# A fused layer kernel on one core: the second half of y is transposed into another PSUM bank, and a dozen steps get new places

## Chip, cores and metric

The kernel runs on one core of a Trainium2 chip. The metric is the device time of one launch in microseconds (us). A core has five engines that this text names: TensorE (PE in the profile; PEld are its weight loads), VectorE (DVE), ScalarE (ACT), GpSimd (POOL) and SyncE (SP), which here only issues DMAs. Each runs its own instructions in the order in which they are written. They wait for each other by semaphores.

## What is computed

Three blocks over x of 2 x 2048 tokens by 1024 features, each added to x:

```
x = x + 0.5 * ffn(layernorm(x))
x = x + attn(layernorm(x))
x = x + 0.5 * ffn(layernorm(x))

ffn:   vecs[s,a,r] = A[a,r,:] . x[s]          a = 64 experts, r = 16
       the 4 experts with the largest |vecs[s,a,:]| get route 1/4
       v[s,r] = sum_a routes[s,a] * vecs[s,a,r]
       out = x W^T + bias + sum_a,r routes[s,a] * B[a,:,r] * v[s,r]
attn:  xz = x W_xproj^T -> delta_r (128), B (16), C (16)
       delta = softplus(delta_r W_dt^T + b_dt)
       h_t = exp(delta_t * A) * h_(t-1) + delta_t * B_t * x_t     (1024 features x 16 states)
       y_t = sum_n h_t * C_t ;  out = y + x * D
```

## The kernel before

**Units.** The work is cut into 64 units of 128 tokens by `plan`. A unit of kind 1 is a tile of the first ffn, and a unit of kind 2 is a tile of the last one. Units 0 to 13 are of kind 1, units 14 to 47 alternate (with two of kind 1 in a row at 29 and 30, and at 46 and 47), and units 48 to 63 are of kind 2. Through units 5 to 57 the scan of the middle block runs beside them: 256 groups of 4 scans over 512 tokens, 5 groups in most units and 4 in nine of them (5, 10, 16, 22, 28, 34, 40, 46 and 52). In a unit, a is the unit itself, b the one behind it, and l the one ahead of it.

**The names in a unit.** TensorE makes three products of a 128-token tile, each 48 matmuls of 512 columns, in two halves (nb) and thirds of 8 matmuls: `experts` (pv<-wA,xT), made for b at the end of unit a; `base` (po<-wW,xT); `routed` (po<-wB,uT). ScalarE squares the expert vectors (`squares`, L773), VectorE adds them up (`sums`, L998) and finds the four largest (`choose`), ScalarE writes the mask (L777), and VectorE forms the gathered and masked vectors (`gather`, L1014 to L1025, through pv). SyncE turns them by DMA into uT (L344). VectorE adds each half of the result to xin (`result`, L1030). For b, VectorE takes the statistics (`unit_stats`, L971), ScalarE normalises (xn, L760), TensorE transposes xn into bank 0 of pv and into pt (`norm_blocks`, L481), ScalarE rounds these to xT's high part (`high`, L765), and VectorE takes the low part (`low_part`, L994). `experts(b, nb=0)` waits with its first third for both high parts and the first low part, and with its last third for the second low part.

**Kind 1 has more.** Its result is normalised again at the end of the unit (`stats("ln2")`, `normed2`, L783). In the next unit, where it is l and called late, TensorE transposes this into pt (`scan_blocks`), multiplies it with wx (`scan_products`, L616, into bank 0 of pv), and transposes the product (`turn_products`, L622).

**Kind 2 takes y.** Where b is of kind 2, TensorE transposes the y that the scan made for it in two halves (`y_blocks`), and VectorE adds each to xin (`add_y`, L980). This is so in units 13, 15, 17, 19, 21, 23, 25, 27, 30, 32, 34, 36, 38, 40, 42, 44 and 47 to 62.

**The scan.** ScalarE makes one decay tile for each scan (L843, `decays`; decay i waits until scan i-2 is done, since pA has two banks), VectorE scans (L1050), GpSimd multiplies by B before (L444, L449) and by C behind it (L457), and TensorE sums over states (`states`, L647). Every 16 scans need a delta tile: `z` (L634) on TensorE, `magnitudes` and `softplus` on ScalarE, `delta` (L1037, L1040; it reads a tile of x that SyncE loads) on VectorE, `delta_copy` (L825) and `delta_out` (L834) on ScalarE, a store to DRAM and loads from there. `plan` gives z to places 0 and 1 of a unit. Units 5, 10, 15, 20, 25, 30, 34, 39, 44, 49 and 54 have both (double units below). Of the other scan units, 6, 7, 11, 12, 16, 17, 21, 26, 31, 35, 36, 40, 41, 45, 46, 50 and 55 have place 1 alone, unit 57 has none, and the rest have place 0 alone.

All places within a unit are written out by hand, engine by engine: `decays(lo, hi)` and `scans(lo, hi)` say which scans of the unit stand there, and the other calls stand between them.

## Time and profile before

| | before |
|---|---|
| median of 3 runs (lowest to highest) | 2925.07 us (2923.59 to 2925.81) |
| the profiled execution | 2920.77 us, span 2919.0 us |
| mean granted TensorE clock | 0.976 |

The rows further down come from the one profiled execution. Its span is the time from the first to the last instruction. The time that the runs report has 1.77 us around it. Rows of the timeline give the start in us from the span's start, the duration in us, the engine, the line, the operation and how many instructions were merged; where the engine stood idle ahead of it, the idle time and what ended it stand in brackets.

### The profile page before, as it was taken

Reading aid. Unit: us, or ns where it says so; the run is one execution under the profiler, and the core shown is the slowest. Engines: PE = TensorE matmul, PEld = TensorE weight load, DVE = VectorE, ACT = ScalarE, POOL = GpSimd, SP = SyncE. Lnnn points to the kernel's source line nnn. Section 1 sums busy time; section 2 is a strip of 40 time slices with the busy share of each in tenths; the row PEclk is TensorE's granted clock in tenths of the full one; section 3 lists DMA queues with packets and bytes.
Section 4 is the critical chain, followed back from the end, with each engine's and each line's share of the span. In section 5 each row is a group of like instructions: output and inputs, shape, how many; then the busy total and the mean of one; then the engine's idle time right before and its main releaser. Section 6 shows DMA issues by size and latency. Waiting matters only on the chain.

```text
span 2919.0 us, 38379 instructions
## 1 busy us (share of the span) xinstructions
PE 2621.1 (90%) x13056; PEld 1164.8 (40%) x13120; DVE 2278.2 (78%) x2917; ACT 1425.2 (49%) x2819; POOL 2347.1 (80%) x703
## 2 busy tenths in 40 slices
PE   4997999999889898889899899899899888988999
PEld 1453444444343344344334334344334333333444
DVE  8435888788878879888888888888797888888533
ACT  5224565555545455554555555555555544454211
POOL 2003999899989999999899899989999899989200
PEclk8999999999999999999999999999999999999999
DMA  5225445544445445544454345344544444344221
GB/s 212 59 61 128 129 132 134 162 139 131 130 136 159 113 122 145 153 126 131 131 163 141 116 126 171 115 135 129 156 136 146 123 147 144 107 133 120 66 58 51
DMA packets 309370, 373.42 MB, mean 128 GB/s; under 512 B 148147, under 2 KB 224051, under 8 KB 309174
## 3 DMA queue, kind: packets, MB, share of 16 engines
q1 hardware_dynamic: 292278, 337.40, 39.2%
q10 hardware_dynamic: 16896, 33.56, 3.8%
q8 instruction: 104, 1.70, 0.2%
q14 instruction: 92, 0.75, 0.1%
HBM read 234.05 MB, written 103.29 MB: 116 GB/s over the span
## 4 chain that ended last, share of the span: by engine, by line
PE 18%; DVE 18%; DVEq 8%; DMA 7%; issue 4%; ACT 4%; POOL 3%; SPq 1%; ACTq 1%; POOLq 0%
DVE mreg L1050 9%; PE po L489 5%; PE pv L489 5%; PE pv L493 3%; PE po L493 3%; DVEq L1052 2%; DMA delta_scratch<-mreg 2%; DMA xin<-x_scratch 2%; DVE pv L1017 2%; DMA mreg<-xnT_scratch 2%; POOL mreg L457 2%; ACT pA L843 1%; DVE sel L1025 1%; DVEq L1016 1%; POOL mreg L449 1%
## 5 line engine op out<-in xcount | busy, mean ns | idle before, releaser
L457 POOL TENSOR_TENSOR mreg<-mreg 128x2048 f32<-128x2048 f32 x256 | 1161.4, 4538 | 30.8 <-DVE hst L1053 30.8
L843 ACT ACTIVATE pA<-mreg,nA 128x512 f32<-128x512 f32 x1024 | 696.1, 687 | 745.9 <-DVE mreg L1050 658.9
L449 POOL TENSOR_TENSOR mreg<-mreg 128x1024 f32<-128x1024 f32 x340 | 795.2, 2364 | 285.3 <-DMA mreg<-delta_scratch 276.6
L1050 DVE TENSOR_TENSOR_SCAN mreg<-pA,hst,mreg 128x512 f32<-128x512 f32 x768 | 941.5, 1265 | 55.1 <-ACT pA L843 43.8
L489 PE MATMUL pv<-wA,xT 128*128 128x512 f16 x2016 | 465.8, 385 | 51.8 <-DVE xT L994 24.4
L489 PE MATMUL po<-wB,uT 128*128 128x512 f16 x2016 | 463.8, 381 | 24.6 <-DVE xin L980 13.1
L489 PE MATMUL po<-wW,xT 128*128 128x512 f16 x2016 | 467.2, 380 | 8.0 <-issue 7.0
L444 POOL TENSOR_TENSOR mreg<-mreg 128x2048 f32<-128x2048 f32 x86 | 390.3, 4539 | 4.1 <-issue 4.1
L489 PEld LDWEIGHTS pv<-wA,xT 128*128 128x128 f16 x2016 | 195.2, 99 | 334.0 <-issue 63.1
L1050 DVE TENSOR_TENSOR_SCAN mreg<-pA,cst,mreg 128x512 f32<-128x512 f32 x256 | 313.5, 1265 | 17.9 <-ACT pA L843 17.6
L489 PEld LDWEIGHTS po<-wB,uT 128*128 128x128 f16 x2016 | 190.8, 98 | 318.8 <-issue 77.0
L998 DVE TENSOR_REDUCE n<-sel 128x32 f32<-128x512 f32 x128 | 85.3, 684 | 263.1 <-ACT sel L773 262.8
L489 PEld LDWEIGHTS po<-wW,xT 128*128 128x128 f16 x2016 | 197.9, 98 | 222.1 <-issue 8.5
L647 PE MATMUL py<-mreg,Em 128*32 128x512 f32 x2048 | 274.5, 608 | 13.0 <-POOL mreg L457 12.4
L493 PE MATMUL pv<-wA,xT 128*128 128x512 f16 x1008 | 244.3, 386 | 22.1 <-DVE xT L994 22.1
L493 PE MATMUL po<-wW,xT 128*128 128x512 f16 x1008 | 253.3, 397 | 0.0
L493 PE MATMUL po<-wB,uT 128*128 128x512 f16 x1008 | 239.9, 381 | 0.0
L1030 DVE SCALAR_TENSOR_TENSOR xin<-po,sc,xin 128x512 f32<-128x512 f32 x128 | 94.5, 738 | 87.1 <-PE po L493 83.2
L493 PEld LDWEIGHTS pv<-wA,xT 128*128 128x128 f16 x1008 | 99.1, 99 | 147.1 <-issue 33.5
L493 PEld LDWEIGHTS po<-wW,xT 128*128 128x128 f16 x1008 | 97.3, 101 | 151.1 <-issue 59.1
L493 PEld LDWEIGHTS po<-wB,uT 128*128 128x128 f16 x1008 | 99.0, 98 | 106.0 <-issue 1.7
L773 ACT ACTIVATE sel<-pv 128x512 f32<-128x512 f32 x128 | 72.3, 584 | 131.3 <-PE pv L493 131.2
(129 smaller groups left out, 2387.5 us busy)
## 6 DMA issues: line engine op xcount, KB each, us to landing
mreg<-delta_scratch SPq DMA_DIRECT2D x256, 512.0 KB, 5.7
delta_scratch<-mreg ACTq DMA_DIRECT2D x128, 256.0 KB
xin<-x SPq DMA_DIRECT2D x32, 512.0 KB, 4.6
x_scratch<-xin SPq DMA_DIRECT2D x32, 512.0 KB, 7.4
xnT_scratch<-auxs SPq DMA_DIRECT2D x32, 512.0 KB, 2.9
mreg<-xnT_scratch SPq DMA_DIRECT2D x64, 256.0 KB, 6.9
mreg<-bc_scratch SPq DMA_DIRECT2D x64, 256.0 KB, 6.0
yT_scratch<-mreg SPq DMA_DIRECT2D x64, 256.0 KB, 2.3
```

The costliest lines, as they stand in the source:

```text
L444: pool.tensor_tensor(Hr[:, G % NH, :, :], u, b.broadcast_to([P, 4, CT]), ALU.mult).then_inc(s_bm, 2)
L449: pool.tensor_tensor(Hr[:, G % NH, 2 * h:2 * h + 2, :], u, b.broadcast_to([P, 2, CT]), ALU.mult).then_inc(s_bm, 1)
L457: pool.tensor_tensor(h, h, Cr[:, g, :].unsqueeze(1).broadcast_to([P, 4, CT]), ALU.mult).then_inc(s_cm, 1)
L489: last = nc.tensor.matmul(dst, lhs[:, 0, k, :], w[:, wb, k, nb * HF:(nb + 1) * HF], start=(first and k == 0 and wb == 0), stop=False)
L493: last = nc.tensor.matmul(dst, lhs[:, 1, k, :], w[:, 0, k, nb * HF:(nb + 1) * HF], start=False, stop=(stop and k == KD - 1))
L647: last = nc.tensor.matmul(py[32 * s:32 * s + 32, :], Em[:, :], Hr[:, G % NH, s, :], start=(g == 0), stop=(g == 3), tile_position=(0, 32 * s))
L773: nc.scalar.activation(sel[:, nb * HF:(nb + 1) * HF], pv[:, nb, :], ACT.Square).then_inc(s_sq, 1)
L843: nc.scalar.activation(pA[:, i % 2, :], Dr[:, 2 * (n % NPR) + i % 2, :], ACT.Exp, scale=nA[:, c:c + 1]).then_inc(s_dA, 1)
L998: V.tensor_reduce(n2[:, nb * NE // 2:(nb + 1) * NE // 2], sel3[:, nb * NE // 2:(nb + 1) * NE // 2, :], AX.X, ALU.add)
L1017: V.tensor_reduce(pvs, sel[:, :].rearrange("p (a r) -> p r a", r=R16), AX.X, ALU.add)
L1030: V.scalar_tensor_tensor(dst, po[:, nb, :], sc[:, 3:4], dst, ALU.mult, ALU.add).then_inc(s_res, 1)
L1050: V.tensor_tensor_scan(h, pA[:, i % 2, :], h, before, ALU.mult, ALU.add).then_inc(s_sc, 1)
```

## The change

There are two parts. The second half of y goes to bank 0 of pv instead of pt, so it no longer waits for the first `add_y` (s_ya) but for the unit's `gather` (s_u), which uses that bank. `scan_products`, which writes that bank too, waits for both `add_y` where there is a y. And a dozen calls stand at new places on TensorE, ScalarE and VectorE.

```diff
+        pty = (pt[:, :], pv[:, 0, :])
...
                 else:
-                    pe.wait_ge(s_ya, b.v * 2 + 1)
-                blocks(pt, lambda k: auxy[:, half * KB + k, :], s_yT, idf[:, :])
+                    pe.wait_ge(s_u, b.u * 2)
+                blocks(pty[half], lambda k: auxy[:, half * KB + k, :], s_yT, idf[:, :])
...
TensorE, unit():
-                z(a, 0)
                 if late:
                     scan_blocks(late, 1)
+                z(a, 0)
                 base(a, 1, 0)
                 if y:
                     if late:
                         pe.wait_ge(s_nc, late.w * 2 + 2)
                     y_blocks(y, 0)
-                if late:
-                    scan_products(a, late)
-                base(a, 1, 1)
                 if y:
                     y_blocks(y, 1)
+                base(a, 1, 1)
                 base(a, 1, 2)
                 states(a, 1)
+                if late:
+                    scan_products(a, late, y)
...
+                routed(a, 0, 0)
                 if late:
                     turn_products(late)
-                routed(a, 0, 0)
                 routed(a, 0, 1)
...
ScalarE, unit():
-                decays(2, 3)
                 if late:
                     scan_input_copies(late, 1)
-                decays(3, 4)
+                decays(2, 4)
                 magnitudes(a, 0)
+                decays(4, 7)
                 softplus(a, 0)
-                decays(4, 8)
+                decays(7, 8)
                 if late:
                     projections(late)
                 decays(8, 9)
+                delta_copy(a, 0)
                 if late:
                     projection_copies(late)
                 decays(9, 10)
-                delta_copy(a, 0)
                 delta_out(a, 0)
...
+                if b:
+                    squares(b, 0)
                 decays(19, 20)
                 if a.kind == 1:
                     normed2(a, a.u * 2 + 4)
                 decays(20, 22)
-                if b:
-                    squares(b, 0)
...
VectorE, unit():
-                scans(4, 7)
+                scans(4, 5)
                 if b and b.kind == 2:
                     add_y(b, 1)
+                scans(5, 7)
                 delta(a, 0)
                 scans(7, 10)
                 if b:
                     unit_stats(b)
-                scans(10, 12)
                 result(a, 0)
-                scans(12, 15)
+                scans(10, 14)
                 if b:
                     low_part(b, 0)
+                scans(14, 15)
                 delta(a, 1)
+                scans(15, 16)
                 if b:
                     low_part(b, 1)
-                scans(15, 17)
+                scans(16, 18)
                 result(a, 1)
-                scans(17, 18)
                 delta(a, 2)
                 if a.kind == 1:
                     ...
                     stats("ln2", xin[:, a.p, :], s_mv2)
+                if b:
+                    sums(b, 0)
                 scans(18, 20)
-                if b:
-                    sums(b, 0)
```

TensorE, middle of a unit whose b is of kind 2 (uT is here the buffer that holds y, L481 before and L482 now its transposes). Before:

```order
L489 MATMUL po<-wW,xT 128x512 x8
L481 MATMUL pt<-idf,uT 128x128 [waits s_ldy]
L481 MATMUL pt<-idf,uT 128x128 x3
L489 MATMUL po<-wW,xT 128x512 x8
L481 MATMUL pt<-idf,uT 128x128 [waits s_ya]
L481 MATMUL pt<-idf,uT 128x128 x3
L493 MATMUL po<-wW,xT 128x512 x8
L647 MATMUL py<-mreg,Em 32x512 [waits s_y,s_cm]
L647 MATMUL py<-mreg,Em 32x512 x3
L489 MATMUL po<-wB,uT 128x512 [waits s_uc0,s_ya]
```

and now:

```order
L490 MATMUL po<-wW,xT 128x512 x8
L482 MATMUL pt<-idf,uT 128x128 [waits s_ldy]
L482 MATMUL pt<-idf,uT 128x128 x3
L482 MATMUL pv<-idf,uT 128x128 [waits s_u]
L482 MATMUL pv<-idf,uT 128x128 x3
L490 MATMUL po<-wW,xT 128x512 x8
L494 MATMUL po<-wW,xT 128x512 x8
L650 MATMUL py<-mreg,Em 32x512 [waits s_y,s_cm]
L650 MATMUL py<-mreg,Em 32x512 x3
L490 MATMUL po<-wB,uT 128x512 [waits s_uc0,s_ya]
```

The second four transposes moved ahead of the second third of base, and their wait is for the gather.

TensorE, the same stretch of a late unit, from the half of base on. Before:

```order
L567 MATMUL po<-brow,onesb 128x512 [waits s_res]
L489 MATMUL po<-wW,xT 128x512 x8
L616 MATMUL pv<-wx,auxs 128x160 [waits s_u,s_nc]
L616 MATMUL pv<-wx,auxs 128x160 x7
L489 MATMUL po<-wW,xT 128x512 x8
L493 MATMUL po<-wW,xT 128x512 x8
L647 MATMUL py<-mreg,Em 32x512 [waits s_y,s_cm]
L647 MATMUL py<-mreg,Em 32x512 x3
L622 MATMUL pv<-idf,xn 128x128 [waits s_pk,s_nc]
L623 MATMUL pv<-idf,xn 32x128
L489 MATMUL po<-wB,uT 128x512 [waits s_uc0]
```

and now:

```order
L568 MATMUL po<-brow,onesb 128x512 [waits s_res]
L490 MATMUL po<-wW,xT 128x512 x16
L494 MATMUL po<-wW,xT 128x512 x8
L650 MATMUL py<-mreg,Em 32x512 [waits s_y,s_cm]
L650 MATMUL py<-mreg,Em 32x512 x3
L619 MATMUL pv<-wx,auxs 128x160 [waits s_u,s_nc]
L619 MATMUL pv<-wx,auxs 128x160 x7
L490 MATMUL po<-wB,uT 128x512 [waits s_uc0,s_nc]
L490 MATMUL po<-wB,uT 128x512 x7
L625 MATMUL pv<-idf,xn 128x128 [waits s_pk]
L626 MATMUL pv<-idf,xn 32x128
```

The product with wx moved behind base and states, and the turning of its result behind the first third of routed.

VectorE, behind the statistics for b (L1050 and L1054 are the scans, L994 and L998 the low parts, L1030 and L1034 the two results, L1062 and L1066 a sum for y). Before:

```order
L973 BN_AGGR ln_mv<-ln_st 128x2
L1050 SCALAR_TENSOR_TENSOR mreg<-pA,hst,mreg 128x512 [waits s_dA] x2
L1053 TENSOR_REDUCE hst<-mreg 128x4
L1030 SCALAR_TENSOR_TENSOR xin<-po,sc,xin 128x512 [waits s_out]
L1050 SCALAR_TENSOR_TENSOR mreg<-pA,hst,mreg 128x512 [waits s_dA,s_sv,s_bm]
L1050 SCALAR_TENSOR_TENSOR mreg<-pA,hst,mreg 128x512 [waits s_dA] x2
L994 TENSOR_TENSOR xT<-pv,xT 128x512 [waits s_xhi]
L994 TENSOR_TENSOR xT<-pt,xT 128x512 [waits s_xhi]
L1050 SCALAR_TENSOR_TENSOR mreg<-pA,hst,mreg 128x512 [waits s_dA]
L1053 TENSOR_REDUCE hst<-mreg 128x4
```

and now:

```order
L977 BN_AGGR ln_mv<-ln_st 128x2
L1034 SCALAR_TENSOR_TENSOR xin<-po,sc,xin 128x512 [waits s_out]
L1054 SCALAR_TENSOR_TENSOR mreg<-pA,hst,mreg 128x512 [waits s_dA] x2
L1057 TENSOR_REDUCE hst<-mreg 128x4
L1054 SCALAR_TENSOR_TENSOR mreg<-pA,hst,mreg 128x512 [waits s_dA,s_sv,s_bm]
L1054 SCALAR_TENSOR_TENSOR mreg<-pA,hst,mreg 128x512 [waits s_dA]
L998 TENSOR_TENSOR xT<-pv,xT 128x512 [waits s_xhi]
L1054 SCALAR_TENSOR_TENSOR mreg<-pA,hst,mreg 128x512 [waits s_dA] x2
L1057 TENSOR_REDUCE hst<-mreg 128x4
L998 TENSOR_TENSOR xT<-pt,xT 128x512 [waits s_xhi]
```

The first low part stands one scan earlier, the second one scan later, and the first result two scans earlier.

## Rows read from the trace of the kernel before

**Rows 1.** The page's parts 1 and 2: busy us, share, instructions; granted clock
```profile
PE 2621.1 (90%) x13056; PEld 1164.8 (40%) x13120; DVE 2278.2 (78%) x2917; ACT 1425.2 (49%) x2819; POOL 2347.1 (80%) x703
...
PEclk8999999999999999999999999999999999999999
```

**Rows 2.** The page's part 4, the chain that ended last, by engine
```profile
PE 18%; DVE 18%; DVEq 8%; DMA 7%; issue 4%; ACT 4%; POOL 3%; SPq 1%; ACTq 1%; POOLq 0%
```

**Rows 3.** Waits, whole span: waiting instruction, releaser; total us, times, longest
```profile
POOL mreg L449 <- DMA mreg<-delta_scratch: 276.6, 29, 175.3
...
PE pt L481 <- DVE xin L980: 55.8, 23, 4.7
...
DVE mreg L1040 <- DMA mreg<-xnT_scratch: 52.6, 11, 5.9
PE pv L616 <- DVE sel L1025: 49.4, 30, 4.0
...
PE pv L489 <- DVE xT L994: 24.4, 22, 1.2
...
PE pv L489 <- ACT xT L765: 23.6, 12, 2.4
...
PE pv L481 <- ACT xn L760: 20.9, 15, 10.0
...
DVE xin L980 <- DMA xin<-x_scratch: 17.0, 6, 6.3
...
DVE mreg L1050 <- POOL mreg L449: 9.2, 8, 2.1
```

**Rows 4.** Timeline of unit 24, a late unit of kind 2 with z at place 0
```profile
1139.93 0.26 ACT L777 ACTIVATE mask<-n2m 128x64 f32<-128x64 f32 x1 [1.70 <-DVE n2m L1009]
...
1148.50 2.41 PE L616 MATMUL pv<-wx,auxs 128*128 128x160 f32 x16 [1.54 <-DVE sel L1025]
...
1163.73 1.25 ACT L760 ACTIVATE xn<-xin,ln_nm,ln_r 128x1024 f32<-128x1024 f32 x1
...
1165.68 3.64 DVE L1050 TENSOR_TENSOR_SCAN mreg<-pA,hst,mreg 128x512 f32<-128x512 f32 x3 [0.53 <-ACT pA L843]
...
1168.16 0.59 ACT L765 ACTIVATE xT<-pt 128x512 f16<-128x512 f32 x1
...
1170.04 3.61 PE L489 MATMUL pv<-wA,xT 128*128 128x512 f16 x16 [0.99 <-DVE xT L994]
...
1182.79 0.26 ACT L777 ACTIVATE mask<-n2m 128x64 f32<-128x64 f32 x1 [1.59 <-DVE n2m L1009]
```

**Rows 5.** Timeline of unit 23, of kind 1, whose b takes y
```profile
1105.41 0.66 PE L481 MATMUL pt<-idf,uT 128*128 128x128 f32 x4 [3.17 <-DVE xin L980]
...
1118.85 1.24 ACT L760 ACTIVATE xn<-xin,ln_nm,ln_r 128x1024 f32<-128x1024 f32 x1
...
1120.14 0.66 PE L481 MATMUL pv<-idf,xn 128*128 128x128 f32 x4 [0.70 <-ACT xn L760]
...
1134.80 1.24 ACT L783 ACTIVATE xn<-xin,ln_nm,ln_r 128x1024 f32<-128x1024 f32 x1
...
1137.17 1.05 ACT L773 ACTIVATE sel<-pv 128x512 f32<-128x512 f32 x2
```

**Rows 6.** Timeline of unit 25, a double unit of kind 1
```profile
1201.85 0.58 ACT L825 ACTIVATE mreg<-pv 128x512 f32<-128x512 f32 x1
...
1220.55 0.69 DVE L1040 TENSOR_TENSOR mreg<-pv,mreg 128x512 f32<-128x512 f32 x1 [4.43 <-DMA mreg<-xnT_scratch]
```

**Rows 7.** Timeline of unit 2, ahead of the scan
```profile
142.62 2.41 PE L616 MATMUL pv<-wx,auxs 128*128 128x160 f32 x16 [0.61 <-DVE sel L1025]
```

**Rows 8.** Timeline of unit 60, behind the scan
```profile
2795.88 1.22 DVE L1025 TENSOR_TENSOR sel<-mask,pv 128x1024 f16<-128x1024 f32 x1
...
2798.49 2.62 SPq L344 DMA_TRANSPOSE uT<-sel  x2
...
2801.86 3.61 PE L489 MATMUL po<-wB,uT 128*128 128x512 f16 x16 [1.72 <-DMA uT<-sel]
```

More of the change, by code:

```diff
@@ L607, in scan_blocks, with scan_products @@
                 blocks(pt, lambda k: xn[:, (half * KB + k) * P:(half * KB + k + 1) * P], s_nT, idf[:, :])
-            def scan_products(a, l):
+            def scan_products(a, l, y):
+                if y:
+                    pe.wait_ge(s_ya, y.v * 2 + 2)
                 if l.w == 0:
@@ L694, in unit @@
                 routed(a, 1, 2)
+                states(a, 3)
                 z(a, 2)
-                states(a, 3)
                 if b:
@@ L885, in unit @@
                     normed(b, 2 * (a.f1s - (a.kind == 1)))
-                decays(12, 14)
+                decays(12, 13)
+                decays(13, 14)
                 magnitudes(a, 1)
@@ L979, in add_y @@
                 dst = xin[:, b.p, half * HF:(half + 1) * HF]
-                V.tensor_tensor(dst, pt[:, :], dst, ALU.add).then_inc(s_ya, 1)
+                V.tensor_tensor(dst, pty[half], dst, ALU.add).then_inc(s_ya, 1)
             def unit_stats(b):
@@ L1106, in unit @@
                     stats("ln2", xin[:, a.p, :], s_mv2)
-                scans(18, 20)
                 if b:
                     sums(b, 0)
+                scans(18, 20)
             def combine():
```

## The prediction, made before the changed kernel was run

> **What bounds the kernel now.** I read the page first. TensorE has the most busy time, 90% of the span, and GpSimd and VectorE have 80% and 78% [rows 1]. The weight loads, at 40%, are no limit. GpSimd's 2347.1 us over 256 groups are 9.17 us a group, so 45.8 us for a unit with five groups. The granted clock is at its upper level nearly throughout [rows 1], so it gives the change nothing to win.
>
> The chain that ended last comes second: TensorE and VectorE have 18% of it each, GpSimd 3% [rows 2]. So no engine bounds the whole. A unit is a loop: mask, gather, ten scans, statistics, xn, transposes, high and low parts, experts for b, squares, the next mask. What stands last in that loop decides.
>
> The waits come third, with the two that the change is aimed at: TensorE waits 55.8 us for the first `add_y` before it turns the second half of y, and 49.4 us for the gather before the product with wx [rows 3]. I then followed one unit of each sort along the timeline to see what becomes of that time.
>
> *Late unit of kind 2* (unit 24, 42.86 us from mask to mask). TensorE waits 1.54 us at L616. But xn is done at 1163.73 + 1.25 = 1164.98, and TensorE takes it in its next matmuls at once. The next three scans end at 1169.32, the low parts follow, and experts start at 1170.04 after a wait of 0.99 for the first of them [rows 4]. TensorE's lost time at L616 has therefore only 0.3 us to give; xn comes from VectorE and ScalarE.
>
> *Unit of kind 1 with y* (unit 23). TensorE loses 3.17 us at the second half of y, and still waits 0.70 us for xn, which ends at 1120.09 [rows 5]. The end of the unit is set by the second normalisation: it ends at 1136.04, two decays follow, then both squares at 1137.17 [rows 5]. TensorE's experts had ended before that. So this unit is VectorE's and ScalarE's.
>
> *Double unit* (unit 25). The copy of the first delta ends at 1202.43, its store has to land, SyncE loads the second z's tile only behind that, and VectorE stands 4.43 us before L1040 [rows 6]; over the kernel it is 52.6 us in 11 double units [rows 3].
>
> **The change part by part.**
>
> *y's second half in pv, product with wx behind base and states.* In unit 23 TensorE would wait for the end of the gather, some 1.5 us, instead of 3.17, and its matmuls up to xn come some 2 us earlier. In late units the 1.6 us on average (49.4 / 30) go. What is behind both is the wait for xn, which grows by as much: before xn, VectorE's work between gather and statistics is the same two additions, one delta and eight scans in another order. I take 0 for all scan units; if that cover were gone, the price would be the 105 us of the two waits, less the new wait of 1.5 us in 30 units or so, which gives 60.
>
> Ahead of the scan there is no such cover: TensorE hardly waits there, and 0.61 us at L616 go in units 1 to 4 [rows 7]. That is 2.4 us. Behind the scan, in units 58 to 62, the turning into uT was issued at 2798.49, behind the second half of y, and routed waits 1.72 us for it [rows 8]. Now the gather's last write ends at 2795.88 + 1.22 = 2797.10, four transposes of some 0.6 us follow, and SyncE issues at 2797.8. That is 0.65 us sooner in 5 units, so 3.3 us.
>
> *The first low part one scan earlier.* In unit 24 it could start when the scan before the third ends, 1.2 us sooner (3.64 / 3), so at 1168.1. The second high part runs from 1168.16 to 1168.75 [rows 4] and experts want it too; the first one ends just ahead of it, and the low part behind that takes some 0.7 (as L1040 does, 0.69 [rows 6]) and ends at 1168.9. With 0.2 from there to the first matmul, experts start at about 1169.1 instead of 1170.04: 0.9 us. It counts only where experts set the end of the unit (kind 2), and only where no softplus lies between the two high parts. With z at place 1 the second high part comes later and already is what TensorE waits for (12 waits, 23.6 us, against 22 of 1.1 us for the low part [rows 3]). So it counts in 14 units: 14, 18, 22, 24, 28, 33, 37, 43, 48, 51, 52, 53, 56, 57. 14 x 0.9 = 12.6 us.
>
> *The second low part one scan (with place 1: two scans and a delta) later.* It is wanted by the third 3.6 us behind the start of experts [rows 4]. From 1168.3 on VectorE has 0.6 + 1.2 + 1.4 + 0.6 = 3.8 us until it ends, 1172.1, and TensorE wants it at 1172.7. With z at place 1, experts start later by the softplus (1.4), and the low part by a delta (1.4), which leaves some 0.4 us. I take 0. In the double units of kind 2 (20, 39, 49, 54) it is late by a scan, but TensorE then also waited there for the copy of delta, which comes sooner by that scan; 0.
>
> *One square and one sum ahead of the last scans.* In kind 1, both squares (1.05 us) stood behind the second xn. Now one stands there, which saves 0.5 us. Against it, VectorE waits some 0.3 for the high part, and the second statistics come later by that. My count of unit 23 gives a mask between 0 and 0.5 us earlier. In 20 single units of kind 1 I take 0.12 each, 2.5 us; both ends, 0 and 10, go to the range.
>
> *The copy of delta ahead of decay 9.* The store is issued some 0.5 us sooner, since ScalarE copies (0.58, [rows 6]) while it would wait for scan 7. The stand before L1040 ends sooner by that, in 7 double units of kind 1: 3.5 us. In the four of kind 2 the later low part takes it.
>
> *What takes back.* A shorter loop moves towards GpSimd, whose pace does not change. VectorE waits little for it now (9.2 us), but it waits 6 times, 17.0 us, for an xin that SyncE issues behind loads which wait for GpSimd [rows 3]. Where units before that got shorter, this wait grows by as much. I take 4 us.
>
> Sum: 12.6 + 2.5 + 3.5 + 2.4 + 3.3 - 4 = 20.3 us. The profiled execution took 2920.77 us, so 2900.5. The median of the three runs lies 4.3 us above it; from it the forecast is 2904.8 us.
>
> **The Trainium skill on this.** The page Perfetto Trace Analysis (Identifying the Most-Contended Engine) says to go by occupancy and to optimise the engine that has most of it, but it warns that busy matmul time is a poor measure, and to take the weight loads' share. By its strategy one closes the gaps on that engine; that is the first rival below, and by it the sum would be some 60 us larger. The trace agrees with the warning: 90% and 40% stand side by side.
>
> **The rivals.**
>
> *TensorE is the bound after all.* Its 90% speak for it. Against it are 0.70 us of wait for xn in unit 23 even after the 3.17. It would give about 60 us and the 20 of my sum, and GpSimd's waits bound it, since its work does not shrink: 276.6 - 175.3 = 101.3 us for delta, apart from the longest, which is the one ahead of the scan [rows 3]. Time: 2845 to 2870. Chance 0.09. A part of it, 30 to 50 us less than before, because the earlier turning lets SyncE go on sooner to the loads: 2875 to 2893, chance 0.16.
>
> *GpSimd takes it all back.* Unit 24, with five groups, already took 2.9 us less than the 45.8 that GpSimd needs for them, and only longer units make up for it. If the scans come to wait for GpSimd as soon as a unit is shorter, only the 5.7 us outside the scan stay. 2919 to 2925, chance 0.13. Against it stand the 101.3 us that it waits for delta.
>
> *The second low part is late (slower).* In 28 units with z at place 1 (17 single and 11 double) it has 0.4 us of slack by my count, behind a delta that waits for ScalarE. If delta ends over 0.4 us later than I think, TensorE stands before its last third, and so does ScalarE, where the square now stands ahead of decay 19: a scan and a delta wait of 1.4 us each. 28 x 1.4 = 39, less the 20 of my sum: 2944. Chance 0.09. From 0.7 us of wait per unit on (20 / 28) it makes the kernel slower.
>
> **How the numbers follow.** My case has a chance of 0.53 with 2893 to 2918; the part above 0.16; the whole of TensorE's waits 0.09; GpSimd 0.13; the late low part 0.09. Two runs of this kernel can be told apart from about 0.2%, 5.85 us. Faster by more: 0.53 + 0.16 + 0.09 = 0.78. Same: 0.13. Slower: 0.09. The range of 8 in 10 leaves out the late low part and most of TensorE's case, 2875 to 2922.
>
> **What would show it.** TensorE's waits for xin before the transposes of y and for the gather before the product with wx are gone, and its waits for xn (now 20.9 us [rows 3]) grow by about as much. TensorE's wait for the low part at L489 falls from 24.4 us to under 8. Units like 24 take 42.0 instead of 42.9, and units like 23 stay within 0.5 us. The double units get some 0.5 us shorter. Waits before the last third of experts stay below 30 us. The prediction is wrong if waits for xn do not grow (TensorE was the bound), if VectorE comes to wait for GpSimd by more than 20 us, or if the wait at the last third of experts exceeds 40.

## The result, and the profile after

| | before | changed |
|---|---|---|
| median of 5 runs (lowest to highest) | 2925.81 us (2923.59 to 2929.73) | 2909.53 us (2902.43 to 2911.2) |
| ratio, 95% interval | | 0.9945 (0.9931 to 0.9959) |
| profiled execution's span | 2919.0 us | 2900.6 us |

The change makes the kernel 16 us faster, where 20 were forecast. Timed again later beside the kernel before, it was 12 us faster (ratio 0.9956, 0.9941 to 0.997). The profiled execution of the changed kernel is its fastest run, 7 us below its median; the one of the kernel before is 5 us below its own, so the profiles flatter the difference by some 2 us. A second profile of the changed kernel, taken later, has a span of 2905.0 us; where the two differ, both are told.

The page of the changed kernel, part 1, and the chain that ended last by engine (part 4):

```profile
PE 2629.8 (91%) x13056; PEld 1167.3 (40%) x13120; DVE 2277.7 (79%) x2917; ACT 1422.9 (49%) x2819; POOL 2347.1 (81%) x703
...
PE 29%; DVE 29%; DVEq 12%; DMA 11%; issue 7%; ACT 5%; POOL 5%; SPq 1%; ACTq 1%; POOLq 0%
```

The engines do the same work as in [rows 1], in less time. The shares of [rows 2] add up to only 64% of the span, since that chain could not be followed back to the start; 18% of it each for TensorE and VectorE are 28% of what was followed, so the chain goes through both in equal parts as before (26% and 30% in the second profile). The waits over the whole span, in the form of [rows 3]:

```profile
POOL mreg L450 <- DMA mreg<-delta_scratch: 259.0, 25, 171.6
...
PE pv L482 <- ACT xn L763: 69.0, 38, 10.0
...
DVE mreg L1044 <- DMA mreg<-xnT_scratch: 50.0, 11, 5.9
...
PE pv L490 <- ACT xT L768: 42.2, 27, 3.2
PE pv L494 <- DVE xT L998: 38.0, 12, 5.7
...
PE pv L482 <- DVE sel L1029: 18.2, 20, 1.8
PE po L490 <- DVE xin L984: 16.3, 12, 4.1
...
DVE xin L984 <- DMA xin<-x_scratch: 13.0, 7, 4.1
...
PE pv L490 <- DVE xT L998: 5.4, 16, 1.1
...
DVE mreg L1054 <- POOL mreg L450: 2.8, 5, 1.2
```

The reader is to see where TensorE's time went. Its 55.8 us before the second half of y are gone and 18.2 us for the gather stand there instead. Its 49.4 us before the product with wx are gone too. Its wait for xn grew from 20.9 to 69.0, and the one for the second high part (L490 for L768) from 23.6 to 42.2. Its wait for the first low part fell from 24.4 to 5.4, and the one for the second low part (L494) rose to 38.0; it was 22.1 us in 11 waits before. VectorE hardly waits for GpSimd (2.8 us).

Unit 24 of the changed kernel along the timeline, next to [rows 4]:

```profile
1136.43 0.26 ACT L780 ACTIVATE mask<-n2m 128x64 f32<-128x64 f32 x1 [1.58 <-DVE n2m L1013]
...
1160.22 1.24 ACT L763 ACTIVATE xn<-xin,ln_nm,ln_r 128x1024 f32<-128x1024 f32 x1
...
1164.66 0.59 ACT L768 ACTIVATE xT<-pt 128x512 f16<-128x512 f32 x1
...
1165.63 3.61 PE L490 MATMUL pv<-wA,xT 128*128 128x512 f16 x16 [0.29 <-DVE xT L998]
...
1178.37 0.26 ACT L780 ACTIVATE mask<-n2m 128x64 f32<-128x64 f32 x1 [1.59 <-DVE n2m L1013]
```

xn starts 23.79 us behind the mask, as before (23.80). Experts start 29.20 behind it instead of 30.11, and the unit takes 41.94 us instead of 42.86. The first low part gave 0.9 us, and the 1.5 us that TensorE saved at wx gave nothing.

The units' lengths, summed by sort, show the whole. Each is the time from one mask (L777, now L780) to the next in the profiled execution, in us; the last columns are the differences to the kernel before.

| units | count | before | changed | second profile |
|---|---|---|---|---|
| 0 to 3 | 4 | 146.5 | -2.0 | -2.5 |
| 4 | 1 | 49.7 | -1.6 | -0.2 |
| double, kind 1 | 7 | 360.3 | +5.5 | +0.8 |
| double, kind 2 | 4 | 198.2 | +4.5 | +6.1 |
| place 1 alone, kind 1 | 8 | 368.0 | -3.2 | -3.3 |
| place 1 alone, kind 2 | 8 | 350.0 | -3.0 | +0.3 |
| place 0 alone, kind 1 | 12 | 560.4 | -5.5 | -3.0 |
| place 0 alone or none, kind 2 | 14 | 622.4 | -10.3 | -8.8 |
| 58 to 62 | 5 | 178.0 | -3.0 | -3.1 |

One sort shows what part of such a difference is not the order of the instructions. The place-1 units of kind 2 differ by 3.3 us between the two profiles of one and the same kernel, and all of it lies in units 16 and 26: 43.22 and 43.20 us in the first profile, 44.86 and 44.87 in the second. In the second, TensorE's granted clock falls from 1.00 (2.4 GHz) to 0.50 (1.2 GHz) for a stretch that begins some 12 us behind the mask in each of them; in the first, it stays at 1.00 in both. Where TensorE waits nearly as long at that place in unit 16 and the clock stays at 1.00 (2.20 us in the low part by place, 2.35 in the second profile), the unit takes 43.20. So differences of 1 to 2 us in a single unit can be the clock's.

Unit 46 has its z at place 0, and the table counts it there; the text ahead of the prediction lists it with place 1. The units with a z at place 1 are 27, 16 single and 11 double.

### The profile page after: what moved, and what is told of

It reads as the page before. It is cut to its first block, busy times and chain, and to the rows that moved or that the text cites. A ratio compares the mean times of both kernels' runs of the same rounds, so it can differ in the third digit from the quotient of the medians.

```text
span 2900.6 us, 38379 instructions
## 1 busy us (share of the span) xinstructions
PE 2629.8 (91%) x13056; PEld 1167.3 (40%) x13120; DVE 2277.7 (79%) x2917; ACT 1422.9 (49%) x2819; POOL 2347.1 (81%) x703
## 4 chain that ended last, share of the span: by engine, by line
PE 29%; DVE 29%; DVEq 12%; DMA 11%; issue 7%; ACT 5%; POOL 5%; SPq 1%; ACTq 1%; POOLq 0%
DVE mreg L1054 13%; PE pv L490 9%; PE po L490 7%; PE pv L494 5%; DVEq L1056 5%; DMA delta_scratch<-mreg 4%; PE po L494 4%; DVE pv L1021 3%; DMA mreg<-xnT_scratch 3%; POOL mreg L450 3%; ACT pA L846 3%; DVE sel L1018 2%; DVEq L1026 2%; DVE sel L1029 2%; DMA xin<-x_scratch 2%
## 5 line engine op out<-in xcount | busy, mean ns | idle before, releaser
L1054 DVE TENSOR_TENSOR_SCAN mreg<-pA,hst,mreg 128x512 f32<-128x512 f32 x768 | 944.9, 1268 | 47.3 <-ACT pA L846 44.7
L490 PE MATMUL pv<-wA,xT 128*128 128x512 f16 x2016 | 469.9, 387 | 47.6 <-ACT xT L768 42.2
L490 PE MATMUL po<-wB,uT 128*128 128x512 f16 x2016 | 473.5, 384 | 24.5 <-DVE xin L984 16.3
L490 PE MATMUL po<-wW,xT 128*128 128x512 f16 x2016 | 461.3, 379 | 8.0 <-issue 7.0
L490 PEld LDWEIGHTS pv<-wA,xT 128*128 128x128 f16 x2016 | 196.8, 100 | 332.8 <-ACT xT L768 87.1
L1054 DVE TENSOR_TENSOR_SCAN mreg<-pA,cst,mreg 128x512 f32<-128x512 f32 x256 | 314.6, 1268 | 16.1 <-ACT pA L846 15.8
L490 PEld LDWEIGHTS po<-wB,uT 128*128 128x128 f16 x2016 | 191.8, 99 | 314.0 <-issue 78.7
L490 PEld LDWEIGHTS po<-wW,xT 128*128 128x128 f16 x2016 | 197.5, 98 | 232.4 <-issue 13.1
L494 PE MATMUL pv<-wA,xT 128*128 128x512 f16 x1008 | 247.7, 390 | 38.0 <-DVE xT L998 38.0
L494 PE MATMUL po<-wB,uT 128*128 128x512 f16 x1008 | 252.8, 396 | 0.0
L494 PE MATMUL po<-wW,xT 128*128 128x512 f16 x1008 | 238.7, 380 | 0.0
L494 PEld LDWEIGHTS pv<-wA,xT 128*128 128x128 f16 x1008 | 98.5, 99 | 166.8 <-issue 58.3
L1034 DVE SCALAR_TENSOR_TENSOR xin<-po,sc,xin 128x512 f32<-128x512 f32 x128 | 92.2, 720 | 84.1 <-PE po L494 79.6
L494 PEld LDWEIGHTS po<-wW,xT 128*128 128x128 f16 x1008 | 94.3, 98 | 149.7 <-issue 44.4
L494 PEld LDWEIGHTS po<-wB,uT 128*128 128x128 f16 x1008 | 102.4, 102 | 114.8 <-issue 16.4
```

The costliest lines, as they stand in the source:

```text
L490: last = nc.tensor.matmul(dst, lhs[:, 0, k, :], w[:, wb, k, nb * HF:(nb + 1) * HF], start=(first and k == 0 and wb == 0), stop=False)
L494: last = nc.tensor.matmul(dst, lhs[:, 1, k, :], w[:, 0, k, nb * HF:(nb + 1) * HF], start=False, stop=(stop and k == KD - 1))
L1034: V.scalar_tensor_tensor(dst, po[:, nb, :], sc[:, 3:4], dst, ALU.mult, ALU.add).then_inc(s_res, 1)
L1054: V.tensor_tensor_scan(h, pA[:, i % 2, :], h, before, ALU.mult, ALU.add).then_inc(s_sc, 1)
```

## The experiments

Each kernel was timed in 5 rounds beside the kernel before; the ratio is to that. TensorE's part alone, and the low parts alone, back and by place ran on one chip; the changed kernel again, the square, the copy and the store on one; the two others on one. The low part by place and the store first are attempts at a better kernel as well.

### TensorE's part alone

TensorE's code is that of the changed kernel; ScalarE and VectorE keep their order, except that the second `add_y` reads its half from pv. Against the kernel before, apart from TensorE's unit(), y_blocks and scan_products, which are those of the change:

```diff
+        pty = (pt[:, :], pv[:, 0, :])
...
-                V.tensor_tensor(dst, pt[:, :], dst, ALU.add).then_inc(s_ya, 1)
+                V.tensor_tensor(dst, pty[half], dst, ALU.add).then_inc(s_ya, 1)
```

> The kernel before with TensorE's part of the change alone: y's second half in bank 0 of pv and TensorE's new order; ScalarE and VectorE keep their old order. My theory (the loop through VectorE and ScalarE sets the scan units, so TensorE's saved waits turn into waits for xn): units of kind 2 with z at place 0 stay at 42.9 us from mask to mask, the gain is only ahead of and behind the scan, -5 to -6 us, ratio 0.998. Rival (TensorE is the bound): it carries most of the measured gain, -12 us or more, ratio 0.996 or less, and units like 24 get shorter than 42.9.

Measured: 2931.49 us, ratio 1.0023 (1.0013 to 1.0034). It is slower than the kernel before. Units like 24 stayed at 42.86, and units 0 to 3 and 58 to 62 gained 2.5 and 3.2 us, as expected. But units 13, 30, 47 and 48 took 15.1 us more together (209.5 instead of 194.4). These four are late and have a y as well. The timeline of unit 13 in this kernel, TensorE, ScalarE and VectorE in turn:

```profile
642.29 4.12 PE L619 MATMUL pv<-wx,auxs 128*128 128x160 f32 x16 [3.90 <-DVE xin L983]
...
646.44 0.30 ACT L797 ACTIVATE xn<-pv 128x160 f32<-128x160 f32 x1 [5.18 <-PE pv L619]
...
647.46 1.28 DVE L1053 TENSOR_TENSOR_SCAN mreg<-pA,hst,mreg 128x512 f32<-128x512 f32 x1 [2.41 <-ACT pA L846]
```

The product with wx now waits for both `add_y`, since the second half of y lies in its bank. ScalarE stands before the projections for it, in front of its next decays, and VectorE's scan waits for the decay. TensorE's wait for xin before routed rose as well, from 13.1 to 65.3 us, while its wait for xn rose only from 20.9 to 29.8: most of the saved time turned up before routed. So neither theory had it whole: TensorE is not the bound, and its part of the change costs time without a second one. The units of kind 2 with place 1 alone took 7.0 us more and the double units other than 30 took 2.0; the causes of these were not told apart.

### The second add_y with it

Against the kernel above, on VectorE:

```diff
-                scans(4, 7)
+                scans(4, 5)
                 if b and b.kind == 2:
                     add_y(b, 1)
+                scans(5, 7)
```

> TensorE's part of the change alone, as in the run that came out slower than the kernel before, and with it one thing on VectorE: the second add_y stands ahead of scans 5 and 6 instead of behind them. Theory (TensorE's new order makes a late unit's product with wx wait for both add_y and routed for the second one, and ScalarE then stands before the projections with its decays behind it; units 13, 30, 47 and 48 paid 3.1 to 5.1 us each): this place takes 2.4 us off each of these waits, units 13, 30, 47 and 48 come back to within 2 us of the kernel before, ratio 0.998 to 1.000. Rival (the slowdown has another cause on TensorE): the ratio stays at 1.002.

Measured: 2921.75 us, ratio 0.999 (0.9979 to 1.0001). Units 13, 30, 47 and 48 take 194.3 us together, as before the change (194.4), and the wait before routed fell to 19.3 us. That theory holds. TensorE's wait for xn is 72.9 us in this kernel. The ratio can't be told from 1. What stays are the 2.5 and 3.2 us ahead of and behind the scan, and against them losses in units of kind 2, 9.9 us in sum. Unit 18 takes 46.98 us instead of 44.49. It does so in the changed kernel too (45.46, second profile 46.72), where its rows for TensorE, ScalarE and VectorE are:

```profile
875.76 2.72 PE L490 MATMUL po<-wB,uT 128*128 128x512 f16 x8 [3.34 <-DMA uT<-sel]
...
878.94 0.28 ACT L802 ACTIVATE auxs<-pv 128x128 f32<-128x128 f32 x1 [2.92 <-PE pv L626]
...
880.26 1.28 DVE L1054 TENSOR_TENSOR_SCAN mreg<-pA,hst,mreg 128x512 f32<-128x512 f32 x1 [2.17 <-ACT pA L846]
```

The turned product now stands behind a third of routed, and routed waits for uT's DMA; when that comes late, ScalarE and VectorE wait with it. The third itself takes 2.72 us for 8 matmuls that take 1.89 in other units: the granted clock falls to 0.50 within it, at 876.68. The turned product was never moved alone, so its share is read from these rows and not shown by a run.

Units 52 and 53 lose by the clock as well. Below is TensorE from the transposes of xn on in unit 52 of the changed kernel:

```profile
2456.84 0.96 PE L482 MATMUL pv<-idf,xn 128*128 128x128 f32 x4 [3.39 <-ACT xn L763]
2457.60 1.06 PE L482 MATMUL pt<-idf,xn 128*128 128x128 f32 x4
2458.45 2.89 PE L494 MATMUL po<-wB,uT 128*128 128x512 f16 x8
```

and in the same unit of the kernel with the low parts alone (next section), which has TensorE's old order:

```profile
2484.24 0.66 PE L481 MATMUL pv<-idf,xn 128*128 128x128 f32 x4 [1.05 <-ACT xn L760]
2484.74 0.60 PE L481 MATMUL pt<-idf,xn 128*128 128x128 f32 x4
2485.18 1.89 PE L493 MATMUL po<-wB,uT 128*128 128x512 f16 x8
```

In both, xn starts 25.50 us behind the mask and the transposes 26.80. With the new order TensorE has stood 3.39 us before them instead of 1.05, and its granted clock is 0.50 from 2457.05 to 2460.4; with the old one it stays at 1.00. Experts then start 32.22 us behind the mask instead of 30.90, and the unit takes 44.97 us instead of 43.64. Unit 53 does the same (44.58 and 43.29). All eight profiles that have both TensorE's new order and the second `add_y` moved show this in both units (44.94 to 45.00 and 44.55 to 44.64); the kernel with TensorE's part back, below, does not (43.64 and 43.34). A long wait is not followed by the lower clock each time: before xn in unit 23 TensorE waits 3.05 us in the changed kernel, and the clock falls at 26.5 us behind the mask; with the copy of delta back it waits 3.04, and the clock stays at 1.00.

### The low parts alone

Against the kernel before, on VectorE:

```diff
-                scans(12, 15)
+                scans(12, 14)
                 if b:
                     low_part(b, 0)
+                scans(14, 15)
                 delta(a, 1)
+                scans(15, 16)
                 if b:
                     low_part(b, 1)
-                scans(15, 17)
+                scans(16, 17)
```

> The kernel before with only the two low parts at their new places. My theory: 14 units of kind 2 without z at place 1 get 0.9 us shorter each (-12.6), units 16, 26, 31 and so on with place 1 alone do not change, and the double units get 1 to 2 us longer each through the second low part behind one more scan (+11 to +20). Sum -2 to +7 us. Rival (the low parts do not matter, the 0.9 us come from TensorE's earlier turning of y and wx): units like 24 stay at 42.9, ratio 1.000, and the double units do not change either.

Measured: 2926.73 us, ratio 1.0007 (0.9996 to 1.0018). The 14 units of kind 2 took 11.8 us less (24, 28 and 33 are at 41.94), the double units 12.0 more, place 1 alone in kind 2 took 1.5 less. The first two are as my theory has them, and the third is near it. The other units of kind 1 took 10.1 more, which it had not. A likely reason, not shown, is that the second low part stands ahead of the second statistics there, where experts do not set the end. The profile is one of the slowest of the 12 executions, 4.6 us above their median.

### The low parts back

Against the changed kernel, on VectorE:

```diff
-                scans(10, 14)
+                scans(10, 15)
                 if b:
                     low_part(b, 0)
-                scans(14, 15)
                 delta(a, 1)
-                scans(15, 16)
                 if b:
                     low_part(b, 1)
-                scans(16, 18)
+                scans(15, 18)
```

> The changed kernel with the two low parts back at their old places, behind scan 14 and behind delta. My theory: units like 24 are back at 42.9 (+12.6 against the changed kernel), and the double units lose what they gained in length (-5 to -14). Sum 0 to +8 against the changed kernel, so -9 to -16 against the kernel before. Rival (the double units are longer because of the store of the first delta, not because of the low part): the double units stay as long, and it is 12 us slower than the changed kernel, about -4 against the kernel before.

Measured: 2912.71 us, ratio 0.9964 (0.995 to 0.9978). Against the changed kernel's two ratios, 0.9945 and 0.9956, that is a loss of 6 or 2 us; the intervals overlap, so the loss can't be told from nothing, and the units have to show it. Units like 24 are back at 42.84 to 42.86. The double units came out 1.3 us longer than before the change, instead of 10.0 (second profile 6.9). So my theory holds and the rival does not: the later low part makes the double units long.

### The low part by place

Against the changed kernel, on VectorE:

```diff
                 scans(14, 15)
                 delta(a, 1)
+                if b and 1 in a.zs:
+                    low_part(b, 1)
                 scans(15, 16)
-                if b:
+                if b and 1 not in a.zs:
                     low_part(b, 1)
```

> The changed kernel, but where the unit has a z at place 1 the second low part stands directly behind delta, ahead of scan 15; elsewhere as in the changed kernel. My theory (in double units the low part is late by a scan, 1.4 us): TensorE's waits before the last third of experts fall from 38 us to about 22, the 11 double units get 1 to 1.4 us shorter each, -11 to -15 against the changed kernel. Rival (the store of the first delta lands late and sets the double units): within 3 us of the changed kernel.

Measured: 2902.71 us, ratio 0.9934 (0.9917 to 0.9951). The double units are 11.0 us shorter than in the changed kernel's first profile, 7.9 than in its second, and 1 us shorter than before the change. The kernel as a whole shows less of it: the kernel with both low parts back, on the same chip, took 10.0 us more, but the changed kernel's two ratios are only 3 and 6 us above this one and their intervals overlap with its own. In the profiles, the other units take 10 us more than in the changed kernel's first profile and 3 us more than in its second. The chain can be read in the timeline of unit 34: VectorE's wait for the tile (L1044), the second low part (L998) and TensorE's last third (L494). First the changed kernel:

```profile
1636.24 0.69 DVE L1044 TENSOR_TENSOR mreg<-pv,mreg 128x512 f32<-128x512 f32 x1 [4.76 <-DMA mreg<-xnT_scratch]
...
1638.29 0.68 DVE L998 TENSOR_TENSOR xT<-pt,xT 128x512 f16<-128x512 f32 x1
...
1639.12 1.89 PE L494 MATMUL pv<-wA,xT 128*128 128x512 f16 x8 [2.88 <-DVE xT L998]
```

And this one:

```profile
1630.73 0.69 DVE L1044 TENSOR_TENSOR mreg<-pv,mreg 128x512 f32<-128x512 f32 x1 [3.53 <-DMA mreg<-xnT_scratch]
1631.34 0.68 DVE L998 TENSOR_TENSOR xT<-pt,xT 128x512 f16<-128x512 f32 x1
1632.16 1.89 PE L494 MATMUL pv<-wA,xT 128*128 128x512 f16 x8 [1.89 <-DVE xT L998]
```

From L1044 to the low part it is 2.05 us in the changed kernel and 0.61 here: the scan and its reduction, 1.44 us. Both numbers are the same in each of the 11 double units. TensorE's waits before the last third fall from 38.0 to 26.0 us, where about 22 were expected.

### The changed kernel again

> The changed kernel once more, to have it on the same chip as the three below and to have a second profile. Every theory: ratio to the kernel before 0.9945 within its interval, double units (sum of 11) 10 us longer than before, units of kind 2 without place 1 at 41.95 us.

Measured: 2909.38 us, ratio 0.9956 (0.9941 to 0.997). Its profile is the second one of the table above. The double units are 6.9 us longer than before, not 10.

### The first square and sum back

Against the changed kernel, on ScalarE; VectorE's `sums(b, 0)` goes back behind `scans(18, 20)` likewise:

```diff
-                if b:
-                    squares(b, 0)
                 decays(19, 20)
                 if a.kind == 1:
                     normed2(a, a.u * 2 + 4)
                 decays(20, 22)
+                if b:
+                    squares(b, 0)
```

> The changed kernel with the first square and the first sum back behind the last scans. My theory (each unit of kind 1 ends with both squares and sums behind the second xn): some 0.5 us more in each of the 27 units of kind 1 in the scan, and nothing in kind 2, so +10 to +14 us against the changed kernel. Rival (other waits cover it, the units of kind 1 owe their few us to something else): within 3 us of the changed kernel.

Measured: 2918.72 us, ratio 0.9988 (0.9977 to 0.9998). That is 9.3 us more than the changed kernel on the same chip (2909.38), near my theory and far from the rival. In a unit of kind 1 the time from the start of the second xn to the next mask is 5.13 us here and in the kernel before, and 4.53 in the changed kernel (medians over the 20 single units; the averages are 5.15, 5.31 and 4.55). So the move is worth 0.60 us in each unit of kind 1. In the changed kernel the second xn itself starts 0.33 us later on average, 41.44 us behind the mask instead of 41.11 (41.56 in the second profile).

### The copy of delta back

Against the changed kernel, on ScalarE:

```diff
-                delta_copy(a, 0)
                 if late:
                     projection_copies(late)
                 decays(9, 10)
+                delta_copy(a, 0)
                 delta_out(a, 0)
```

> The changed kernel with the copy of delta back behind decay 9. The store of the first delta was issued 1.2 us sooner in the changed kernel's double units (18.3 instead of 19.5 us behind the mask) and landed no sooner (28.5 both), since it took 10.3 us instead of 9.05. Theory one (the store of the y tile, which SyncE now issues 0.8 us behind it instead of just ahead of it, shares its way): issued later it takes 9.0 us again and lands at 28.5, so within 2 us of the changed kernel. Theory two (the store is slower in the changed kernel for another reason): it still takes over 10 us and lands at 29.7, the double units get 1.2 us longer each, +13.

Measured: 2907.25 us, ratio 0.9949 (0.9934 to 0.9963), 2 us from the changed kernel on the same chip. Theory one holds. Below are, in the timeline of unit 34 of the changed kernel, ScalarE's issue of the delta store (ACTq), SyncE's store of the y tile (SPq L336), and SyncE's next issue (L308), which waits for the delta store:

```profile
1615.11 1.09 ACTq L837 DMA_DIRECT2D delta_scratch<-mreg  x2
...
1615.92 0.37 SPq L336 DMA_DIRECT2D yT_scratch<-mreg  x1
1626.55 1.18 SPq L308 DMA_DIRECT2D mreg<-delta_scratch  x2
```

and in the same unit with the copy back:

```profile
1619.44 0.38 SPq L336 DMA_DIRECT2D yT_scratch<-mreg  x1
...
1619.83 1.11 ACTq L837 DMA_DIRECT2D delta_scratch<-mreg  x2
...
1629.31 1.18 SPq L308 DMA_DIRECT2D mreg<-delta_scratch  x2
```

The landing is read from SyncE's next issue, which starts as soon as the store is through. From issue to landing it is 11.4 us where the tile's store comes 0.8 us behind, and 9.5 where it comes 0.4 us ahead. On average over the 11 double units: 10.34 us and 9.00. Unit 5, which has no y tile to store, takes 8.7 us in the changed kernel too. So the store was issued 1.2 us sooner and landed at 28.55 us behind the mask instead of 28.48.

### The store of delta first

Against the kernel with the low part by place, on ScalarE:

```diff
                 delta_copy(a, 0)
+                delta_out(a, 0)
                 if late:
                     projection_copies(late)
                 decays(9, 10)
-                delta_out(a, 0)
```

> The kernel with the low part by place (second low part directly behind delta where z is at place 1), and both the copy and the store of the first delta ahead of decay 9 and of the projection copies. If the landing of the store sets the double units: issued another 1.2 us sooner, at 17.2 us behind the mask, most of it is through before the y tile's store starts, it lands at 26.5 to 27.8, and the 11 double units get 1 us shorter each: -8 to -12 against the low part by place, so 0.990 of the kernel before. If something else sets it (the load of the tile, or a fixed end of all stores), nothing changes: 0.9934.

Measured: 2896.72 us, ratio 0.9921 (0.9907 to 0.9936). The store is issued at 17.5 us behind the mask, the tile's store comes 1.5 us behind it, it takes 9.7 us and lands at 27.1 instead of 28.5. The double units are 13.0 us shorter in sum than with the low part by place, 14 us shorter than before. It beats the kernel before by 0.8% and, on the same chip, the changed one by 12.7 us. The 0.990 that was expected was not reached. Against the low part by place (ratio 0.9934, another chip) the intervals overlap, and the two profiles' spans are 2899.8 and 2899.0 us (the former is 5 us above its kernel's median). Units 14, 24, 28 and 33, which have place 0 alone, take 42.5 to 42.6 us here instead of 41.9, probably since the store's issue stands ahead of decay 9 there too. No run has the store first in the double units alone.

### TensorE's part back

The changed kernel with TensorE's code, and the bank that the second `add_y` reads, of the kernel before. Apart from TensorE's unit(), y_blocks and scan_products:

```diff
-                V.tensor_tensor(dst, pty[half], dst, ALU.add).then_inc(s_ya, 1)
+                V.tensor_tensor(dst, pt[:, :], dst, ALU.add).then_inc(s_ya, 1)
```

> The changed kernel with TensorE's part undone: y's second half in pt again, TensorE's old order; ScalarE and VectorE in their new order. Theory (within the scan TensorE's part gives nothing where the loop through VectorE and ScalarE sets the unit): the 5 to 6 us ahead of and behind the scan go, units of kind 2 without place 1 stay at 41.95, and the ratio is 0.9965. Rival (with the shorter loop TensorE has become the bound in late units and y units, where it has 1.5 to 3 us less room now): these units get longer too, the whole gain goes, ratio 0.999 or more.

Measured: 2916.85 us, ratio 0.9976 (0.9966 to 0.9986). Units 24, 28 and 33 stay at 41.9, and units 0 to 3 and 58 to 62 are back at their old lengths (differences 0.0 and +0.1). The ratio lies between the two theories: TensorE's part is worth 0.2 to 0.3% in the changed kernel, of which the 5 us outside the scan are the larger share. The rest is in units of kind 1 with place 0, 563.0 us against 555.0 and 557.4, and I didn't tell its cause apart. Units 52 and 53 go the other way: 1.3 us shorter each than in the changed kernel, and the section on the second `add_y` shows why.

## Why the prediction held, and where it did not

*TensorE's waits turn into waits for xn.* Right in its kind, and only half in its size. TensorE's part alone left units like 24 at 42.86. The two old waits, less the new one, are 87 us; the wait for xn grew by 48 of them, not by about as much, and the one for the second high part by 19. In TensorE's part alone it grew by 9, since the time was lost before routed; with the second `add_y` moved it grew by 52. The gain outside the scan was forecast at 2.4 and 3.3 us and came out at 2.0 to 2.5 in units 0 to 3 and 3.0 to 3.1 in units 58 to 62; unit 4 gave 0.2 to 1.6 more. Closing the gaps of the engine with the most occupancy is what the Trainium skill advises (Perfetto Trace Analysis, Optimization Strategy). In this case's trace that did not pay by itself: with the waits that summed to 105.2 us [rows 3] taken out by TensorE's part alone, the kernel was 0.23% slower, as other waits on TensorE came in their place.

*Its cover was taken too simply.* I took TensorE's new order at 0 in all scan units. Two new couplings in it have a price: the product with wx behind both `add_y` (15.1 us in four units, unless the second `add_y` moves too, which the change does), and the turned product behind routed (2.5 us in unit 18 without the low parts, together with the clock there). My count of unit 24 had room for the second, and did not look at units in which uT lands late.

*The granted clock.* The prediction says that it "gives the change nothing to win", and puts nothing for what it could lose. In units 52 and 53 the longer wait for xn was followed by a stretch at half the clock, and cost 1.3 us each.

*The first low part, 14 x 0.9.* The mechanism and its size were right: 0.91 us in each of units 14, 24, 28, 33, 37 and 43 (258.4 to 253.0 us together), and alone it took 11.8 of the 12.6 us. In the changed kernel 8.8 to 10.3 us of it are left: units 52 and 53 take 0.4 us more each instead of 0.9 less, unit 18 takes 1.0 more (2.2 in the second profile), and unit 51 gained 3.1, more than its share.

*The second low part at 0.* This step failed. "In the double units of kind 2 (20, 39, 49, 54) it is late by a scan, but TensorE then also waited there for the copy of delta, which comes sooner by that scan; 0" named the place and gave it no price, and for those of kind 1 I took it not to matter. The double units grew by 6.9 to 10.0 us; the low part by place took 7.9 to 11.0 us off. The waits before the last third were 38.0 us (34.3 in the second profile), over the 30 that the prediction allowed as a sign of being right and just under the 40 that would have shown it wrong. Unit 34 shows how. Before:

```profile
1649.85 1.89 PE L493 MATMUL pv<-wA,xT 128*128 128x512 f16 x8
1650.11 1.24 ACT L783 ACTIVATE xn<-xin,ln_nm,ln_r 128x1024 f32<-128x1024 f32 x1
...
1651.25 1.12 ACT L773 ACTIVATE sel<-pv 128x512 f32<-128x512 f32 x2
```

and in the changed kernel:

```profile
1643.90 1.24 ACT L786 ACTIVATE xn<-xin,ln_nm,ln_r 128x1024 f32<-128x1024 f32 x1
...
1644.30 1.89 PE L494 MATMUL pv<-wA,xT 128*128 128x512 f16 x8
1646.22 0.60 ACT L776 ACTIVATE sel<-pv 128x512 f32<-128x512 f32 x1 [1.08 <-PE pv L494]
```

The masks are at 1604.90 and 1596.65. Before, the last third of experts' second half started 44.95 us behind the mask, the second xn ran from 45.21 to 46.45 and the squares followed it at once, so xn set the end of the unit. In the changed kernel that third started at 47.65, the second xn ended at 48.49, and the last square waited for the third until 49.57, so experts set it. The unit grew by 2.65 us.

*The copy of delta, -3.5.* This failed too. It was issued sooner, by 1.2 us and not 0.5, but it landed no sooner. I priced the issue and not the way: the tile's store, that had been just ahead of it, came to stand in the middle of it.

*One square and one sum, -2.5.* Right in its mechanism, and too small. The term was 0.12 us net in each of 20 units, from 0.5 us saved and some 0.3 lost to a wait; measured were 0.60 saved against 0.33 by which the second xn came later (0.45 in the second profile). In the 20 single units of kind 1 it makes 5.4 us (3.0); they gained 8.7 (6.4) in all, and the rest was not told apart. Put back, it cost 9.3 us in median, and against the second profile the units of kind 1 show it: 11.6 us in the single ones and 6.4 in the double ones, which I had not counted. The other sorts differ in both directions (double units of kind 2 5.6 less, single ones of kind 2 at place 0 or without z 3.3 more, at place 1 3.3 less).

*What takes back, +4.* This was not seen: VectorE's waits for xin were 13.0 and 16.8 us, against 17.0, and those for GpSimd 2.8 us, against 9.2.

The errors went against each other. By the sorts of the first profile they are +13.5 us for the double units (low part and copy), +2.3 for the first low part, -6.2 for kind 1, -3.0 for place 1 in kind 2, -4 for what was to take back, and -0.9 outside the scan: +1.7 on a forecast of -20.3, and the units' sum is -18.6. On the second profile the same terms are +10.4, +3.8, -3.8, +0.3, -4 and -0.1, so +6.6 and a sum of -13.7. The medians of the two timings are at -16 and -12. That the sum came within 4 us on the first was in part luck: two failed steps on the double units, 10.4 to 13.5 us together, were offset by gains in kind 1 that were too small in the forecast and by a price that did not come.

## What to carry to other kernels

Follow one unit of each sort along the timeline before pricing a wait: the sum of an engine's waits says nothing until it is known what stands behind them, and here 105 us of TensorE's waits were worth 5 us outside the scan, and nothing in units like 24. When an engine's step moves, check every unit sort in which its result is wanted late, not the common one; moving the two low parts was worth -0.9 us in one sort and +1 in another, and placing the second one by sort took the +1 away. When a DMA is issued sooner, look at which other transfer it now meets; its landing is the number that counts. Look at the granted clock where an engine's wait was moved: a pause that costs nothing by itself can be followed by a slower stretch that does.

## What the hardware showed that I had not expected

The two 256 KB stores of delta took 9.0 us on average from issue to landing when a 256 KB store with a median of 2.3 us was issued 0.4 us ahead of them, and 10.3 us when it was issued 0.2 to 0.8 us behind the first of them. Alone, in unit 5, they took 8.7 to 8.9 us in the same kernels. So in these runs a short store ahead cost the long ones next to nothing, and one just behind their issue cost them 1.3 us on average.

With the store first, where the short one came 1.5 us behind, they took 9.7 us on average: 9.4 in seven of the ten units that have one, and 10.3 to 10.5 in units 25, 34 and 54. But there unit 5, which has none, took 9.5 us as well. So the short store can't be what makes these longer than 8.9; another transfer that the earlier issue meets is a likely cause, and no run shows which.

TensorE's granted clock shows two levels in these traces, 1.00 and 0.50, and where it fell decided what it cost: with xn and its transposes at the same times, the lower level from the transposes on made units 52 and 53 1.3 us longer, and one some 12 us behind the mask went with 1.6 us more in units 16 and 26 from one execution of the same kernel to the next.
